# Splitting the expert weights on ScalarE and GpSimd instead of GpSimd alone, with the stage orders redone

## What is computed

```
x = x + tanh(g0) * cross_attention_0(layernorm(x), ctx, mask)   # "A": 4 heads, rotary
x = x + tanh(g1) * fp4_ffn(layernorm(x))                        # "F": blockwise FP4 quantise, 704 wide
x = x + tanh(g2) * cross_attention_1(layernorm(x), ctx)         # "B": 16 heads
z = layernorm(x); route each token to its top 2 of 8 experts    # "R"
x = x + tanh(g3) * sum_e w_e * ((silu(z@W1[e]+b1[e]) * (z@W2[e]+b2[e])) @ W3[e] + b3[e])
```

## Time and profile before

| what | us |
|---|---|
| median of 3 runs (lowest, highest) | 1921.44 (1916.14, 1923.22) |
| the profiled execution, its span | 1920.27, 1918.6 |
| PE busy | 1572.6 (82%) |
| DVE busy | 1236.2 (64%) |
| ACT busy | 738.9 (39%) |
| POOL busy | 643.7 (34%) |

### The profile page before, as it was taken

One profiled execution on the slowest core, in us unless ns is written; L12 is line 12 of the kernel. 1 busy time (PEld: TensorE's weight loads), 2 busy tenths in 40 slices (PEclk: granted clock), 3 DMA queues, 4 the chain that ended last, 5 costly groups with the idle time before them and its releaser, 6 DMA issues.

```text
span 1918.6 us, 36797 instructions
## 1 busy us (share of the span) xinstructions
PE 1572.6 (82%) x12221; PEld 1252.5 (65%) x12222; DVE 1236.2 (64%) x3068; ACT 738.9 (39%) x1545; POOL 643.7 (34%) x624
## 2 busy tenths in 40 slices
PE   2345889888888888897888777737999999999995
PEld 2233567566656666665666555526888888888884
DVE  5757788778888888788788765423444444444442
ACT  0011334444444444344444433203444554445542
POOL 0001234244233423433342343313344434434432
PEclk9556899989999989998999988658999999999998
DMA  4001020221122022102201220235422332232223
GB/s 132 11 1 41 11 88 1 90 88 57 34 88 88 2 88 88 60 30 89 88 15 66 80 78 0 78 112 183 153 33 33 99 99 33 33 101 33 33 33 109
DMA packets 63099, 123.78 MB, mean 65 GB/s; under 512 B 13890, under 2 KB 51899, under 8 KB 58811
## 3 DMA queue, kind: packets, MB, share of 16 engines
q1 hardware_dynamic: 45675, 102.75, 15.6%
q0 software_dynamic: 17312, 19.56, 6.3%
HBM read 78.63 MB, written 48.04 MB: 66 GB/s over the span
## 4 chain that ended last, share of the span: by engine, by line
PE 73%; DVE 13%; issue 6%; ACT 4%; DMA 2%; POOL 2%; SPq 0%; DVEq 0%; ACTq 0%; POOLq 0%
PE bank L1243 17%; PE bank L1245 16%; PE bank L1244 16%; PE bank L1315 7%; PE bank L1339 6%; PE bank L1328 4%; PE bank L1407 1%; ACT b_q L736 1%; PE bank L1463 1%; PE bank L1517 1%; DVE b_sx L1008 1%; DVE b_mx L1006 1%; DVE b_rv L926 1%; PE bank L1427 1%; ACT b_pt L684 1%
## 5 line engine op out<-in xcount | busy, mean ns | idle before, releaser
L1243 PE MATMUL bank<-split_room,wm 128*128 128x256 f16 x1152 | 314.7, 273 | 8.5 <-issue 6.9
L1245 PE MATMUL bank<-split_room,wm 128*128 128x256 f16 x1152 | 314.6, 273 | 0.0
L1244 PE MATMUL bank<-split_room,wm 128*128 128x256 f16 x1152 | 314.6, 273 | 0.0
L1220 DVE SCALAR_TENSOR_TENSOR split_room<-bank,b12e,split_room 128x256 f32<-128x256 f32 x288 | 138.1, 483 | 265.1 <-ACT split_room L786 260.1
L786 ACT ACTIVATE split_room<-bank,b12e 128x256 f32<-128x256 f32 x288 | 134.5, 471 | 195.3 <-PE bank L1245 191.3
L1315 PE MATMUL bank<-b_k,b_q 128*128 128x480 f32 x256 | 139.5, 629 | 34.7 <-ACT b_q L736 28.7
L647 POOL DMA_INDIRECT acc<-split_room,m_cur x72 | 115.3, 1602 | 131.7 <-ACT split_room L800 105.9
L1243 PE MATMUL bank<-wm,split_room 128*128 128x256 f16 x576 | 157.0, 273 | 0.0
L1244 PE MATMUL bank<-wm,split_room 128*128 128x256 f16 x576 | 157.0, 273 | 0.0
L1245 PE MATMUL bank<-wm,split_room 128*128 128x256 f16 x576 | 157.0, 273 | 0.0
L1339 PEld LDWEIGHTS bank<-b_v,b_pt 120*128 120x128 f32 x1024 | 132.9, 199 | 36.8 <-issue 30.5
(11 more groups left out here) (352 smaller groups left out, 3984.2 us busy)
## 6 DMA issues: line engine op xcount, KB each, us to landing
split_room<-in_L_ffn_W SPq DMA_DIRECT2D x48, 512.0 KB, 8.0
wsplit<-split_room SPq DMA_DIRECT2D x16, 1536.0 KB, 6.4
wm<-wsplit SPq DMA_DIRECT2D x16, 1536.0 KB, 8.3
acc<-x SPq DMA_DIRECT2D x17, 256.0 KB, 8.2
xin<-in_x SPq DMA_DIRECT2D x16, 256.0 KB
rows<-r_row SPq DMA_DIRECT2D x16, 256.0 KB, 3.0
ct<-in_ctx SPq DMA_DIRECT2D x16, 120.0 KB
cb<-in_ctx SPq DMA_DIRECT2D x16, 120.0 KB, 7.1
```

The source lines that it names most:

```text
L1220: dve.scalar_tensor_tensor(m_h[:, c % 3], bank[c % 4][:, TILE:2 * TILE], b12e[:, p, 1, c:c + 1], m_s[:, c % 2], ALU.add, ALU.mult).then_in ...
L1243: pe.matmul(o, lh, rh, start=start, stop=False)
L1244: pe.matmul(o, ll, rh, start=False, stop=False)
L1245: return pe.matmul(o, lh, rl, start=False, stop=stop)
```

## The change

The high halves are made by ScalarE (a copy that writes f16) and only the low halves by GpSimd. A new semaphore, W.hi, tells GpSimd that a high half is there; W.split now counts three per batch instead of six. The waits for the loads and for the earlier store move from GpSimd to ScalarE. The five lists are redone: the weight stages run for batch s on SP and GpSimd and for batch s-1 on ScalarE, GpSimd's three stages stand together at the end of its list behind R.ln, and several stages of A, B, F and R swap places. The loop covers steps 4 to 13 (five turns) instead of 3 to 14 (six turns).

```diff
-        (W.in_, W.split, W.out) = (
+        (W.in_, W.hi, W.split, W.out) = (
...
-            "SP": ("A.load/-1 W/2 B.out/3 B.load/0 R.rank/3").split(),
-            "POOL": ("B.ln/2 W2/3 R.ln/3 A.ln/-1 F.p0/1 F.p1/1 F.ln/0 R.scatter/3 F.p/0 W0/2 W1/2").split(),
-            "ACT": ("B.t0/3 B.s2/3 B.t1/3 B.t2/3 B.s3/3 F.ht1/2 A.s0/0 B.t3/3 B.s4/3 B.s5/3 A.s1/0 A.t0/0 B.t4/3 B.s6/3 "
-                "B.t5/3 A.t1/0 B.s7/3 B.t6/3 B.t7/3 F.t/1 B.ot/3 F.gu0/1 A.ot/0 F.gu1/1 B.ct/2 B.zt/2 F.gu2/1 R.t/3 "
-                "R.logit/3 F.gu3/1 B.k/2 B.q/2 A.t/-1 B.s0/2 B.s1/2 F.ht0/1").split(),
-            "DVE": ("F.ht0/2 A.rot/0 B.s3/3 A.s0/0 F.ht1/2 B.s4/3 F.ln/1 B.s5/3 A.s1/0 F.z/1 B.s6/3 B.p3/3 F.q/1 B.s7/3 "
-                "A.p0/0 F.d1/2 F.t/1 A.p1/0 B.p7/3 B.ln/2 B.ot/3 B.z/2 F.gu0/1 A.ot/0 B.out/3 R.ln/3 F.gu1/1 R.z/3 "
-                "F.q0a/1 F.gu2/1 A.out/0 B.ct/2 R.t/3 R.logit/3 A.ln/-1 B.zt/2 R.rank/3 F.gu3/1 F.q0b/1 A.z/-1 F.q1a/1 "
-                "F.q0c/1 B.s0/2 A.t/-1 B.v/2 B.s1/2 F.q1b/1 B.s2/2 F.q1c/1").split(),
-            "PE": ("B.p0/3 B.t1/3 B.t2/3 B.s3/3 F.ht1/2 A.s0/0 B.p1/3 B.t3/3 B.s4/3 B.p2/3 A.s1/0 A.t0/0 B.s5/3 F.d0/2 "
-                "B.t4/3 B.s6/3 B.p3/3 A.t1/0 A.p0/0 B.p4/3 B.t5/3 B.s7/3 F.d1/2 B.t6/3 B.p5/3 A.p1/0 B.t7/3 F.t/1 B.p6/3 "
-                "B.p7/3 F.gu0/1 B.ot/3 A.ot/0 B.out/3 F.gu1/1 B.ct/2 A.out/0 B.zt/2 F.gu2/1 R.t/3 R.logit/3 R.rank/3 "
-                "F.gu3/1 B.k/2 B.q/2 B.s0/2 A.t/-1 B.v/2 B.s1/2 A.kv/-1 F.ht0/1 B.t0/2 B.s2/2 A.q/-1").split(),
+            "SP": ("A.load/-1 B.out/3 B.load/0 R.rank/3 W/0").split(),
+            "POOL": ("A.ln/-1 F.p0/1 F.p1/1 R.scatter/3 F.ln/0 F.p/0 B.ln/1 R.ln/2 W0/0 W1/0 W2/0").split(),
+            "ACT": ("B.t2/3 F.ht1/2 B.s3/3 B.t3/3 B.s4/3 A.s0/0 B.s5/3 A.s1/0 A.t0/0 B.t4/3 B.s6/3 B.t5/3 A.t1/0 B.s7/3 "
+                "B.t6/3 B.t7/3 F.t/1 A.ot/0 B.ot/3 W0/1 F.gu0/1 W1/1 W2/1 F.gu1/1 B.ct/2 F.gu2/1 R.t/3 B.zt/2 R.logit/3 "
+                "F.gu3/1 B.k/2 B.q/2 A.t/-1 B.s0/2 B.s1/2 F.ht0/1 B.t0/2 B.s2/2 B.t1/2").split(),
+            "DVE": ("B.s2/3 F.ht0/2 A.rot/0 B.s3/3 A.s0/0 F.ht1/2 B.s4/3 F.ln/1 B.s5/3 A.s1/0 F.z/1 B.s6/3 B.p3/3 F.q/1 "
+                "B.s7/3 A.p0/0 F.d1/2 A.p1/0 F.t/1 B.p7/3 B.ln/2 B.ot/3 B.z/2 A.ot/0 F.gu0/1 B.out/3 A.out/0 R.ln/3 "
+                "F.gu1/1 R.z/3 B.ct/2 F.q0a/1 F.gu2/1 R.t/3 B.zt/2 R.logit/3 A.ln/-1 R.rank/3 A.z/-1 F.gu3/1 F.q0b/1 "
+                "F.q1a/1 F.q0c/1 B.s0/2 A.t/-1 B.v/2 B.s1/2 F.q1b/1 F.q1c/1").split(),
+            "PE": ("A.s0/0 B.p1/3 B.t3/3 B.s4/3 A.s1/0 B.p2/3 B.s5/3 F.d0/2 B.t4/3 A.t0/0 B.s6/3 B.p3/3 A.t1/0 A.p0/0 B.p4/3 "
+                "B.t5/3 B.s7/3 F.d1/2 B.t6/3 B.p5/3 A.p1/0 B.t7/3 F.t/1 B.p6/3 B.p7/3 A.ot/0 B.ot/3 F.gu0/1 B.out/3 "
+                "A.out/0 F.gu1/1 B.ct/2 F.gu2/1 R.t/3 B.zt/2 R.logit/3 R.rank/3 F.gu3/1 B.k/2 B.q/2 B.s0/2 A.t/-1 B.v/2 "
+                "B.s1/2 A.kv/-1 B.t0/2 F.ht0/1 B.s2/2 A.q/-1 B.p0/2 B.t1/2 B.t2/2 B.s3/2 F.ht1/1").split(),
...
-        FIRST_LOOP, END_LOOP, STEPS = 3, 15, NB + max(LAGS)
+        FIRST_LOOP, END_LOOP, STEPS = 4, 14, NB + max(LAGS)
...
-                    if j == 0:
-                        pool.wait_ge(W.in_, b * 48 + 48)
-                        if not isinstance(b, int) or b >= 1:
-                            pool.wait_ge(W.out, b * 16)
-                        pool.sem_inc(ticks, 1)
-                    pool.tensor_scalar(w_hl[:, j, 0], w_st[:, j], 1.0, 1.0, ALU.mult, ALU.mult).then_inc(W.split, 1)
-                    pool.wait_ge(W.split, b * 6 + 2 * j + 1)
+                    pool.wait_ge(W.hi, b * 3 + j + 1)
                     pool.tensor_tensor(w_hl[:, j, 1], w_st[:, j], w_hl[:, j, 0], ALU.subtract).then_inc(W.split, 1)
...
+            def weights(j):
+                def stage(b, p):
+
+                    if j == 0:
+                        held(act, W.in_, b * 48 + 48)
+                        if not isinstance(b, int) or b >= 1:
+                            held(act, W.out, b * 16)
+                    act.activation(w_hl[:, j, 0], w_st[:, j], ACT.Copy).then_inc(W.hi, 1)
+                return stage
```

More of the change, by code:

```diff
@@ L301, in gated_stack @@
         W = Signals()
-        (W.in_, W.split, W.out) = (
+        (W.in_, W.hi, W.split, W.out) = (
             sem(f"w_{n}") for n in (
-                "in_ split out").split())
+                "in_ hi split out").split())
         M = Signals()
@@ L474, in weights @@
                 if not isinstance(b, int) or b >= 1:
-                    sp.wait_ge(W.split, b * 6)
+                    sp.wait_ge(W.split, b * 3)
                     sp.dma_start(w_dst(b - 1), w_hl[:, :, :, :].rearrange("p c h n -> p (c h n)")).then_inc(W.out, 16)
@@ L511, in _ @@
             expert_in(0, 0)
-            sp.wait_ge(W.split, 6 * NB)
+            sp.wait_ge(W.split, 3 * NB)
             sp.dma_start(w_dst(NB - 1), w_hl[:, :, :, :].rearrange("p c h n -> p (c h n)")).then_inc(W.out, 16)
@@ L767, in _ @@
             stages = {"A.t": a_t, "A.ot": out_t(A, a_ot, bank[0]), "F.t": f_t, "F.ht0": f_ht_(0), "F.ht1": f_ht_(1),
-                      "B.zt": b_zt_, "B.ct": b_ct_, "B.k": b_k_, "B.q": b_q_, "B.ot": out_t(B, b_ot, bank[3]), "R.t": r_t, "R.logit": r_logit}
+                      "B.zt": b_zt_, "B.ct": b_ct_, "B.k": b_k_, "B.q": b_q_, "B.ot": out_t(B, b_ot, bank[3]), "R.t": r_t, "R.logit": r_logit,
+                      "W0": weights(0), "W1": weights(1), "W2": weights(2)}
             stages.update(ra)
```

## The result

The changed kernel took 1966.95 us, median of 4 runs (1954.28 to 1977.43), beside 1918.79 for the kernel before, 4 runs (1913.28 to 1923.22): ratio 1.025, 95% interval 1.018 to 1.032. Forecast were 1914 and a range of 1889 to 1937. The profiled execution took 1970.47, its span is 1968.5, and the mean granted clock is 0.878, where it was 0.900. Since the granted clock is either full or half, that is (1 - 0.878) x 2 x 1968.5 = 480 us at half clock against 384. If PE has work all through the 96 us more, they are worth 48 us, which is nearly the whole difference of the two spans (49.9). This is an estimate, and it says what the loss is made of, not where it comes from.

The account below looks back on a forecast made before the run. A step was taken as a chain passing between engines, none full. 14 steps at 0.35 us gave 5 less, step 17 2.6 less, step 2 2 more: 5.6 under the profiled 1920.27, so 1914; range 1889 to 1937.

Parts of the forecast that it names:

- the turn term of the sum: Loop jumps: one turn fewer saves 1.7 us, 0.3 more charged on each of five turns, so nothing remains.
- what would make the forecast fail: Signs against the forecast, among them PE's clock falling longer behind the grown router wait: 1.5 us per step, 21 in all.
- The wait moves from B.z to R.z, and a step gains 0.2: Stretch F.gu0 to F.gu3: b_z freed, R.z held 3.6 us by GpSimd's low halves; F.gu3 starts at 417.3, not 417.47.
- The wait for r_mb: PE's wait for the router's one-hot, in front of R.rank, claimed to grow from 1.8 to about 3 us.
- the walk: One step's stretch from F.gu0 to F.gu3 timed in the new order: F.gu1 starts at 403.9, F.gu3 at 417.3.
- the stretch at 0.50 behind the router: PE's half-clock stretch from 417.4 to 422.1, following the wait for the one-hot, claimed to stay.
- One instruction of R.z free, or both: Rival: GpSimd hardly holds R.z; one instruction free gives 1893 us (chance 0.18), both free 1866 us (0.06).
- POOL does not let go between low halves: Rival: VectorE gets no turn until all three low halves end; F.gu3 1.2 us later, 1934 us in all; chance 0.26.
- Nothing comes of it: Rival: steps are set by something the walk doesn't see, all shifts are slack; within 5 us of before; chance 0.08.
- The rival with both free: Neither R.z instruction held: 3.65 us per step over 14 steps plus 2.6, 54 less, 1866 us; chance 0.06.
- Costs taken as nothing: ScalarE's three copies, about 1.05 us each in its idle time, later loads and store, and the unchanged second part: no cost.

Follow-up runs that it names:

- e7: The changed kernel with all steps of the first part written out, no loop: 1930.32 us, ratio 1.003 to the kernel before.
- e8: The kernel before with all steps of the first part written out, no loop: 1914.05 us, ratio 0.993 to the kernel before.
- e1: The changed kernel with the jump put back to its old place in the lists of PE, DVE and ACT: 1937.45 us, ratio 1.008 to the kernel before.
- e3: The changed kernel with the jump put back in PE's list alone, in front of B.p0: 1935.25 us, ratio 1.007 to the kernel before.
- e4: The kernel before with only its jumps moved to the changed kernel's places: 1960.52 us, ratio 1.018 to the kernel before.
- e9: The kernel before, its loop and PE and DVE lists kept, with high halves on ScalarE and low halves behind R.ln: 1934.43 us, ratio 1.006.
- e10: e7 with low halves behind R.scatter (one) and F.p (two), highs around the router: 1895.77 us, ratio 0.987 to the kernel before.
- e5: e1 with GpSimd's three low halves moved from behind R.ln to behind R.scatter: 1929.85 us, ratio 1.002 to the kernel before.
- e12: The kernel before, loop kept, with highs on ScalarE and low halves behind R.scatter (one) and F.p (two): 1894.57 us, ratio 0.988.
- e2: The changed kernel with the jump put back in DVE's list alone, in front of F.ht0: 1965.30 us, ratio 1.023 to the kernel before.

## Why the prediction was wrong

**The step that failed** is the turn term of the sum. For the new places of the jumps, DVE's in front of B.s2 and PE's in front of A.s0, the prediction had "I charge 0.3 more on five turns, so nothing remains". It saw the places and priced only the idle time. The jumps measured some 29 us instead of 0 (e7 and e8), and their place alone 30 to 37 (e1, e3, e4; in e3 it is PE's only). What the term left out is the half clock behind the stops: 14 to 20 us of it at each jump of the changed kernel in front of A.s0, 3.4 or none at those of e1 and e3 in front of B.p0. The idle time was priced too low as well: 1.3 to 3.4 us in front of A.s0, at three of the four jumps with some 2 more a little before it. That PE's clock may fall for longer stood under what would make the forecast fail, but for the router's wait, not for the turn.

**"The wait moves from B.z to R.z, and a step gains 0.2"** was right in the hold, number by number (b_z, b_rv, r_z, the ScalarE copies, 2.2 in front of R.t, the wait for F.gu0's product gone). Two things in it were off. The wait for r_mb, given as about 3, stayed at 1.9. And the new wait of 1.0 for the product of F.gu1 was not in it: F.gu1 starts some 2 us sooner behind F.gu0 than the walk had it, 5.3 against 7.2. F.gu3 starts 0.7 sooner after F.p. The balance over the whole step was wrong in sign: without jumps a step takes 66.6 instead of 65.9 and the kernel 16 to 19 us more. e9 puts the price of the split with its low halves behind R.ln at 11 to 12 in the old lists, and e10 shows that moving them gives back 31. The likely carrier of this second part is the clock again. The prediction took the stretch at 0.50 behind the router as staying the same. In the one step looked at it is 10 us in e7 and 7 in e8, and over all runs e7 has some 31 us more at half clock. That the held R.z lengthens it is not shown by itself: no run varies the wait with all else kept.

**The rivals.** One instruction of R.z free, or both: no, all 28 take over 2.15. POOL does not let go between low halves: not for R.z; in e5 it did so twice, for an instruction of A.rot, and let the same instruction in elsewhere. Nothing comes of it: no, 48 us. The rival with both free stood 48 below the forecast; moving the low halves gained 31 (e10 against e7) and 36 (e12 against e9) by the ratios, less than that, since r_mb (1.8) and r_zt (1.2) remain as waits.

**Costs taken as nothing** held: the copies on ScalarE (1.05, none waiting for a load), the later transfers, the second part (603.5).

**Open.** Why the clock comes back in 3.4 us at one place and only in 14 to 20 at another is not settled. The place differs in two things at once. The work behind it is another, and PE also stands idle more there: 1.89 and 1.32 us in the changed kernel, 3.94 in e2, 1.20, 1.85 and 2.22 in e4, against 1.96 and 0.86 in e3. e5 has a long stop in front of A.s0 without a jump there, and the same 17 us; but none of the runs varies the length of the stop or the work behind it with all else kept. Nor are the 11 us settled between e9 and before: its jump steps are 2.5 longer and its other steps 0.5 shorter, and no run splits this.

## What to carry to other kernels

Where a hand-written pipeline runs in a hardware loop, the place of the jump in each engine's list is worth a test of its own: price not only the stop, but the clock behind it, and here the place where PE's list begins was the one that mattered. An instruction of GpSimd that holds VectorE is best put where VectorE waits for something else, in small pieces; taking the hold from one instruction and giving it to the next gained nothing here. When several lists are redone at once, run the split and the orders apart: here two losses lay on top of each other, and a gain of 1.2% was there for another place of the low halves.

## What the hardware showed that was not expected

- PE stopped 1.89 us, its granted clock fell to 0.50, it stopped 1.32 more in front of A.s0, and the clock stayed at 0.50, 17 us in all, though PE was busy without a pause in the last 13 of them (8.00 of 8.00 us between 446 and 454). After stops of 1.96 and 0.86 us behind a jump in front of B.p0 it was back after 3.4.
- Back-to-back instructions of GpSimd (2.13 to 2.18 each) let a VectorE instruction in after each one (r_z with one tensor operand, 2.15 to 2.21; in e5 a_k with two, 2.11 and 2.19). Twice in e5 a_k was held over all three (7.08 and 7.09), when it had started 0.65 before the first. The Trainium skill ("SBUF — State Buffer", SBUF: two separate sides) says that the one that starts first keeps the pair for its whole instruction. The r_z rows agree. The two long holds don't come out of it, as far as the low halves go, for there the VectorE instruction is the one that is recorded as starting first.
- A jump back went with stops of PE of 1.3 to 3.4 us and of VectorE of 2.1 to 2.7, and removing all jumps made even the kernel before 0.7% faster.
